# First expert stage: the gate multiplies the input rows, relu goes from PSUM straight to the second product's rows, the bias becomes a weight row, and experts are worked in pairs

## The chip, the core and the metric

The kernel runs on one core of a Trainium2 chip, as one program. The metric is the device time of a launch in microseconds (us). The core has TensorE (PE: matrix products, whose clock is granted at 1.2 or 2.4 GHz), VectorE (DVE), ScalarE (ACT), GpSimd (POOL) and SyncE (SP), which here only issues transfers (DMAs). Each engine runs its own instructions in order and waits on semaphores for the others. SBUF is the memory of 128 partitions that all engines read and write. PSUM is the memory that TensorE writes its products to: eight banks of 128 partitions by 512 f32.

## The reference, cut to what matters

The program is eleven stages of a small model over 8 x 1056 rows of 64 numbers. The fifth, `_L0_ffn_ref`, is a mixture of 16 experts:

```python
gate_logits = x @ gate_w + gate_b                       # 16 logits a row
topk_vals, topk_idx = jax.lax.top_k(gate_logits, 2)
topk_w = jax.nn.softmax(topk_vals, axis=-1)             # two weights a row, both positive
h = jax.nn.relu(jnp.einsum('bsh,ehf->bsef', x, w1) + b1)   # 64 -> 128, each expert
expert_out = jnp.einsum('bsef,efh->bseh', h, w2) + b2      # 128 -> 64
moe = sum over the two chosen experts of weight * expert_out
y = x + moe;  then layer norm with gamma and beta, and the residual
```

Here x is already the layer-normalised input of the stage: its 64 numbers have mean zero in every row.

## The kernel before

The stage is `moe(..., "mo0", relu=True, E=16, ...)`, line 2046. It takes the 8448 rows in MK = 11 blocks of MN = 768 rows. A block is kept as two halves of EN = 384 rows: the 64 numbers of a row of the first half lie on partitions 0 to 63, those of the second half on 64 to 127, the rows along the columns. All experts are computed for all rows; an expert that a row hasn't chosen has weight zero.

For each expert n of a block, four things are done. TensorE makes the hidden numbers (`z`, L2392: two f32 products of 64 rows of weights by 128 columns, 384 columns streamed, one for each half, into two banks). ACT applies relu with the bias b1 and writes `act1` (L2510, 128x768). TensorE spreads the expert's weight over 128 partitions (`spread`, L2427: two bf16 products with a matrix of ones, into banks WB and WB+1). DVE multiplies the two (`g`, L2663, 128x768). Then TensorE multiplies by w2 and adds up over the experts (`down`, L2444, two f32 products of 128 rows of weights by 64 columns, into one bank). In program order TensorE does `up1(n+2)`, `spread(n+1)`, `down(n)`. A block's first expert has six small bf16 products more, for b2 (L2441).

What a block needs besides is placed beside the experts by the table `place`: on DVE the layer norm of the next block (`stats`, `aggregate`, `norm`), its choice of experts (`top`, `gap`, `pick`, `share`, `parts`) and the end of the block before (`add`, `moments`, `end`); on TensorE the turns of rows into columns (`t0` L2357, `w_turn` L2375, `y_turn` L2385) and the logits (L2365); on POOL the roots and the last multiply and adds.

Stages overlap at their ends. While the stage before (`project`, "prj") does its last blocks, SP issues this stage's first loads (`ahead`, which runs `fetch`), on the same queue as that stage's stores. The stage's small constants (`gw`, `sone`, `w2`, `b1`, `b2`) are loaded when SP enters the stage, after the last store of "prj" was issued. In `project`, DVE may write the rows of block b into `hn` only when the store of block b-2 has landed (`back`, L2019), and L1875 is that store. The last expert stage of the program, `expert_units` ("mo1"), has a structure of its own; its lines that matter here are `gates` (L2965, a spread over 64 partitions, 512 columns, both halves into one bank), `third` (L2988) and `gated` (L3151, DVE: input rows times the spread weight).

Of the kernel before, what the change touches and what calls it, by code (L numbers as in the profile page):

```python
# [2045 lines left out]
def moe(nc, a, const, ps, stage, relu, E, h_in, outer, h_out, gate_w, gate_b, norm_w, w1_d, b1_d, w3_d, w2_d, b2_d,  # L2046
        sel_d):
# [3 lines left out]
    hidden = w1_d.shape[1]  # L2051
    NH = -(-hidden // P)
    NW = 1 if relu else 2
    WC = NW * hidden
    E3 = 3 * E
    U = 2
    RING = 2
    assert (U * NH) % RING == 0 and (MK - 3) % U == 0
    if relu:
        place = {"sums": 1, "y_turn": 2, "add": 3, "moments": 4, "end_root": 6, "end": 6, "scale": 7,  # L2060
                 "stats": 0, "aggregate": 1, "root": 3, "norm": 4, "t0": 5, "t0_cp": 6, "logits": 7, "top": 8, "gap": 9,
                 "exp": 11, "pick": 10, "share": 11, "parts": 12, "w_turn": 13, "w_turn_cp": 14}
    else:
        place = {"sums": 1, "y_turn": 1, "add": 2, "end": 4,
                 "stats": 0, "root": 1, "norm": 1, "t0": 3, "t0_cp": 4, "logits": 4, "top": 5, "gap": 5, "exp": 6, "pick": 6,
                 "share": 7, "parts": 7, "w_turn": 8, "w_turn_cp": 9}
    with ExitStack() as ctx:
        nm = Names(nc, ctx, const, stage)
        wf = nm.sb("wf", [P, WC])
        gw = nm.sb("gw", [P, 2, E])  # L2070
        w2 = nm.sb("w2", [P, NH, C])
        sel = nm.sb("sel", [P, NH * P], BF16)
        sone = nm.sb("sone", [P, NH * P])
        iota = nm.sb("iota", [P, E])
        nw = nm.sb("nw", [P, C])
        gb = nm.sb("gb", [P, 2, C])
        gbias = nm.sb("gbias", [P, E])
        b1 = nm.sb("b1", [P, NH])
# [21 lines left out]
        prob = nm.sb("prob", [P, MT, E])  # L2100
        tot = nm.sb("tot", [P, 5, MT])
# [11 lines left out]
        xb = nm.sb("xb", [P, MT, C])  # L2113
# [8 lines left out]
        names = ("blank", "w_in", "gate_in", "vec_in", "rows_in", "e_in", "iota_set", "sel_made",  # L2122
                 "b2_hi", "b2_rest", "st_made", "agg_made", "var_made", "half_set", "rstd_made", "cen_made", "xn_made",
                 "t_mm", "t_cp", "lg_mm", "lg_made", "max_made", "gap_made",
                 "exp_made", "share_made", "stk_made", "wt_mm", "wt_cp", "z_mm", "z3_mm", "wb_mm", "act_made",
                 "sw_made", "g_made", "acc_mm", "y_cp", "yt_mm", "add_made", "end_made", "var2_made", "rstd2_made",
# [4 lines left out]
        WB, SIDE, ACC = 4, 6, 7  # L2131

        def hr(i):
            return min(P, hidden - i * P)

        def steps(eng, step):

            step(0, 0, True, False)
            for it in range(0, (MK - 3) // U):
                for u in range(U):  # L2140
                    step(it * U + (1 + u), (1 + u) % 2, False, False)
            step(MK - 2, MK % 2, False, False)
            step(MK - 1, (MK - 1) % 2, False, True)

        def beside(k, par, first, last, n, end_parts, route_parts):

            for name, part in end_parts:
                if place[name] == n and not first:
                    part(k - 1, 1 - par)
            for name, part in route_parts:  # L2150
                if place[name] == n and not last:
                    part(k + 1, 1 - par)
# [7 lines left out]
        NVEC = 16 * (3 if relu else 1)  # L2160
        NROWS = 16 * (1 + (1 if hidden % P else 0) + (7 if relu else 0))
        NEND = 16 * (2 if relu else 4)
# [1869 lines left out]
```

## Time and profile before

| | |
|---|---|
| median of 3 runs | 2764.04 us (2763.9 to 2764.17) |
| the profiled execution | span 2762.5 us, from its first to its last instruction; 1.5 us less than the median run, which also holds what lies around it |
| share of the span busy | PE 91%, DVE 72%, ACT 54%, POOL 15% |
| the stage | its first hidden product starts at 1362.58 us, its last product ends at about 1720.9 us |
| PE in the stage, 1500 to 1532 us | 31.50 of 32.00 us busy |
| DVE, ACT there | 24.44 and 15.38 of 32.00 us busy |
| granted clock of TensorE | 0.50 until 1368 us, 1.00 from there to the end of the stage |

How to read it: a time is in us from the span's start. A merged row gives the start of the first instruction and the stretch to the end of the last. The ends of products are modelled and overlap the start of the next, so that the distance from one start to the next is the pace, and a busy PE isn't PE at its peak.

### The profile page before, as it was taken

What the parts mean: (1) busy time and instruction counts of PE and PEld (TensorE: products, weight loads), DVE (VectorE), ACT (ScalarE), POOL (GpSimd) and SP (SyncE); (2) the same over time, 40 slices, a digit from 0 to 9 for tenths busy, and PEclk for the clock granted to TensorE, in tenths of its full rate; (3) what the DMA queues carried; (4) which work ended last, traced back from release to release, by engine and by line L of the source; (5) the groups of instructions that cost most, each with busy time, mean ns of one, the idle gap of its engine ahead of it and who ended that gap; (6) DMA issues with size and microseconds to landing.
All of it is one profiled execution on the core that took longest, in us unless ns stands there. A gap on an engine that the chain in (4) does not pass through costs nothing. (4 is left out here: it accounts for less than half of the span.)

```text
span 2762.5 us, 52420 instructions
## 1 busy us (share of the span) xinstructions
PE 2510.6 (91%) x18456; PEld 1101.7 (40%) x18456; DVE 1994.3 (72%) x5104; ACT 1485.0 (54%) x2543; POOL 415.7 (15%) x505
## 2 busy tenths in 40 slices
PE   7887759999999999998699999897789999699999
PEld 3323642333333333333433333566644444433333
DVE  5776769889888988984477776658777675366665
ACT  4322754777777777775144454334756767143443
POOL 1121310000000000003311112223101010411110
PEclk9998767999999999998599999655689999599999
DMA  2001550101010111122500000135532122701110
GB/s 86 16 16 29 179 178 13 34 27 36 25 36 25 36 33 28 36 50 44 115 16 20 18 15 21 47 89 143 189 109 84 63 86 44 151 18 26 31 24 12
DMA packets 233526, 155.21 MB, mean 56 GB/s; under 512 B 187617, under 2 KB 192546, under 8 KB 233042
## 3 DMA queue, kind: packets, MB, share of 16 engines
q1 hardware_dynamic: 220098, 123.57, 16.7%
q0 software_dynamic: 10368, 19.06, 2.4%
q10 hardware_dynamic: 2808, 9.22, 1.5%
q8 instruction: 158, 2.59, 0.4%
q14 instruction: 94, 0.77, 0.1%
HBM read 86.75 MB, written 65.09 MB: 55 GB/s over the span
## 5 line engine op out<-in xcount | busy, mean ns | idle before, releaser
L1758 DVE TENSOR_REDUCE att_mpart<-ps 128x1 f32<-128x512 f32 x1024 | 633.9, 684 | 55.5 <-PE ps L1578 50.4
L1716 ACT ACTIVATE att_p<-ps 128x704 f32<-128x704 f32 x768 | 546.6, 760 | 214.7 <-PE ps L1643 207.6
L1672 PE MATMUL ps<-att_p,att_v 128*9 128x352 f32 x3072 | 300.8, 462 | 0.1
L1578 PE MATMUL ps<-att_kT,att_qT 64*128 64x512 bf16 x1024 | 281.2, 386 | 21.1 <-DMA att_qz<-qt_d 8.4
L1643 PE MATMUL ps<-att_qT,att_kT 64*128 64x352 bf16 x1536 | 251.5, 317 | 7.3 <-ACT att_p L1716 6.9
L1372 DVE TENSOR_REDUCE cau_mpart<-ps 128x1 f32<-128x512 f32 (+5 forms) x384 | 193.2, 553 | 80.8 <-PE ps L1198 60.8
L2510 ACT ACTIVATE mo_act<-ps,mo_b 128x768 f32<-128x768 f32 x176 | 156.3, 901 | 132.3 <-PE ps L2392 128.8
L2663 DVE TENSOR_TENSOR mo_g<-mo_act,ps 128x768 f32<-128x768 f32 x176 | 167.5, 952 | 77.6 <-PE ps L2427 41.5
L1339 ACT ACTIVATE cau_p<-ps 128x704 f32<-128x704 f32 (+6 forms) x272 | 171.5, 660 | 82.4 <-PE ps L1257 49.8
L3062 ACT ACTIVATE mo_act<-ps 128x1024 f32<-128x1024 f32 (+1 forms) x108 | 102.9, 953 | 195.0 <-PE ps L2976 194.7
L1643 PEld LDWEIGHTS ps<-att_qT,att_kT 64*128 64x128 bf16 x1536 | 82.0, 93 | 272.7 <-issue 262.5
L1549 POOL DMA_DIRECT2D o_d<-att_o x128 | 64.1, 508 | 841.1 <-ACT att_o L1699 841.0
L2392 PE MATMUL ps<-mo_x,mo_wf 64*128 64x384 f32 x704 | 162.8, 540 | 0.9 <-issue 0.9
L3173 DVE TENSOR_TENSOR mo_g<-mo_act,ps 128x1024 f32<-128x1024 f32 (+1 forms) x108 | 122.1, 1131 | 50.3 <-PE ps L2988 47.5
L2444 PE MATMUL ps<-mo_g,mo_w 128*64 128x384 f32 x704 | 151.8, 510 | 0.4 <-DVE mo_g L2663 0.4
L1257 PE MATMUL ps<-cau_qT,cau_kT 128*128 128x352 bf16 (+7 forms) x576 | 128.4, 287 | 1.8 <-ACT cau_p L1339 1.5
L1195 PE MATMUL ps<-cau_kT,cau_qT 128*128 128x512 bf16 (+5 forms) x384 | 113.2, 335 | 13.7 <-ACT cau_qT L1314 7.5
L1578 PEld LDWEIGHTS ps<-att_kT,att_qT 64*128 64x128 bf16 x1024 | 87.7, 94 | 93.8 <-issue 53.0
L2988 PE MATMUL ps<-mo_gx,mo_w 64*128 64x512 f32 (+3 forms) x576 | 113.5, 595 | 0.2 <-DVE mo_g L3173 0.2
L599 DVE TENSOR_TENSOR mix_gam<-ps,mix_gamT 128x512 f32<-128x512 f32 x128 | 86.2, 686 | 32.8 <-PE ps L403 32.3
L3000 PE MATMUL ps<-mo_g,mo_w 128*64 128x512 f32 (+1 forms) x432 | 108.8, 582 | 0.4 <-DVE mo_g L3173 0.2
L2976 PE MATMUL ps<-mo_x,mo_w 64*128 64x512 f32 (+1 forms) x432 | 108.8, 581 | 0.0
(448 smaller groups left out, 4271.6 us busy)
## 6 DMA issues: line engine op xcount, KB each, us to landing
qt_d<-pre_qT SPq DMA_DIRECT2D x8, 1056.0 KB, 4.3
kt_d<-pre_kT SPq DMA_DIRECT2D x8, 1056.0 KB, 6.8
att_kT<-kt_d SPq DMA_DIRECT2D x32, 264.0 KB, 2.8
att_qT<-qt_d SPq DMA_DIRECT2D x32, 264.0 KB, 3.0
cqt_d<-cpr_qT SPq DMA_DIRECT2D x8, 1056.0 KB
cau_qT<-cqt_d SPq DMA_DIRECT2D x16, 528.0 KB, 3.9
o_d<-att_o POOLq DMA_DIRECT2D x128, 37.1 KB, 2.7
cv_d<-cpr_v POOLq DMA_DIRECT2D x16, 288.0 KB, 6.0
```

What stands on the lines that cost most here:

```text
L1257: mm = pe.matmul(ps[r0:r0 + kn, at, off:TH], kT[:, u, tile * P:tile * P + kn], qT[:, u, s, q], start=True, stop=m1 <= m0)
L1339: e = act.activation(p[:, n % RING, :, off:TH], ps[:, bank:bank + 2, off:TH], ACT.Exp)
L1372: red = dve.tensor_reduce(mpart[:, j, s, i:i + 1], ps[:, 4 + place, 0:w], AX.X, ALU.max)
L1578: mm = pe.matmul(ps[:, bank, :], qT[half(s), u, j * P:(j + 1) * P], kT[half(s), u, c * BANK:(c + 1) * BANK], start=True, stop=not near)
L1643: mm = pe.matmul(ps[:, bank + s, 0:TH], kT[half(s), u, i * P:(i + 1) * P], qT[half(s), u, cols], start=True, stop=not near)
L1672: mm = pe.matmul(ps[32 * cg:32 * cg + DV, 7, 0:TH], v[:, u, i, s, :], p[:, r, s, :], start=i < 2, stop=i == FULL - 1)
L1716: e = act.activation(p[:, n % PRING, :, :], ps[:, bank:bank + 2, 0:TH], ACT.Exp)
L1758: red = dve.tensor_reduce(mpart[:, j, s, c:c + 1], ps[:, bank, :], AX.X, ALU.max)
L2392: mm = pe.matmul(ps[0:m, bank + s, 0:EN], wf[s * C:(s + 1) * C, w0 + n * P:w0 + n * P + m], x1[s * C:(s + 1) * C, par, :], start=True, sto ...
L2444: mm = pe.matmul(ps[s * C:(s + 1) * C, ACC, 0:EN], w2[0:m, n, :], g[0:m, (par * NH + n) % RING, s, :], start=n == 0 and not relu, stop=n = ...
L2510: act.activation(act1[0:m, r, :, :], ps[0:m, zb:zb + 2, 0:EN], ACT.Relu, bias=b1[0:m, n:n + 1])\
L2663: dve.tensor_tensor(g[0:m, r, :, :], src[0:m, r, :, :], ps[0:m, bank:bank + 2, 0:EN], ALU.mult)\
```

## The change

`moe` is replaced by `relu_units` for this stage. Since the gate weight w of a row is never negative, w * relu(x @ w1 + b1) = relu((w*x) @ w1 + w*b1). So:

- the weight multiplies the 64 input numbers instead of the 128 hidden ones. `gates` spreads it over 64 partitions (48 rows of weights by 64 columns, the two halves of a block into partitions 0 to 63 and 64 to 127 of one bank), for two experts at once, and one DVE instruction (`gated`, 128x768) makes the multiplied rows `gx` of both;
- ACT's relu reads PSUM and writes `g`, which `down` reads: there is no `act1`, no bias operand, and no DVE multiply for each expert;
- b1 enters as a row of the weights. The input's numbers have mean zero, so number 0 is minus the sum of the others: column 0 of `xm` is set to one, w1 rows 1 to 63 get row 0 subtracted, and row 0 is replaced by b1; in the same way for the gate matrix and its bias;
- the loops go over pairs of experts (88 of them). The side work has a table of its own with steps counted in pairs, and bank SIDE is handed round by one order of uses.

```diff
+    place = {"stats": -11, "aggregate": -10, "root": -10, "norm": -9, "t0": -8, "t0_cp": -8, "logits": -7, "top": -7,
+             "gap": -6, "exp": -6, "pick": -5, "share": -5, "parts": -4, "w_turn": -3, "w_turn_cp": -3,
+             "sums": 7, "y_turn": 10, "add": 10, "moments": 11, "end_root": 11, "end": 12, "scale": 12}
...
             for r in (0, C):
-                sp.dma_start(wf[r:r + C, 0:hidden], w1_d).then_inc(S["w_in"], 16)
+                sp.dma_start(w1[r + 1:r + C, :], w1_d[1:C, :]).then_inc(S["w_in"], 16)
+                sp.dma_start(w1[r:r + 1, :], b1_d).then_inc(S["w_in"], 16)
+                sp.dma_start(w0[r + 1:r + C, :], w1_d[0:1, :].broadcast_to([C - 1, E * P])).then_inc(S["w_in"], 16)
...
+            pool.tensor_tensor(gw[:, :, :], gw[:, :, :], g0[:, :, :], ALU.subtract).then_inc(S["gw_made"], 1)
...
+                pool.tensor_tensor(w1[:, cols], w1[:, cols], w0[:, cols], ALU.subtract).then_inc(S["w_made"], 1)
...
+            def gates(m):
+                j, q = divmod(m, PAIRS)
+                if q == 0:
+                    pe.wait_ge(S["side_read"], use_no["w_turn", j] + 1)
+                at_least(pe, S["gx_made"], m)
+                for i in range(2):
+                    e = 2 * q + i
+                    for s in range(2):
+                        mm = pe.matmul(ps[halves(s), GATE + i, 0:EN], sel[s * C:s * C + E3, e * C:(e + 1) * C],
+                                       wT[s * C:s * C + E3, j % 2, :], start=True, stop=True)
+                mm.then_inc(S["gate_mm"], 1)
...
+            def up(m):
+                pe.wait_ge(S["gx_made"], m + 1)
+                for i in range(2):
+                    at_least(pe, S["g_made"], 2 * (m - 1) + i + 1)
...
+                if 0 <= step + 1 < N_PAIRS:
+                    up(step + 1)
+                if 0 <= step + 2 < N_PAIRS:
+                    gates(step + 2)
+                if 0 <= step < N_PAIRS:
+                    down(step)
+                side_parts(step, parts)
...
-                        act.activation(act1[0:m, r, :, :], ps[0:m, zb:zb + 2, 0:EN], ACT.Relu, bias=b1[0:m, n:n + 1])\
-                            .then_inc(S["act_made"], 1)
+                    act.wait_ge(S["z_mm"], 2 * m + i + 1)
+                    act.activation(g[:, m % 2, i, :, :], ps[:, Z[i]:Z[i] + 2, 0:EN], ACT.Relu).then_inc(S["g_made"], 1)
...
-                    dve.tensor_tensor(g[0:m, r, :, :], src[0:m, r, :, :], ps[0:m, bank:bank + 2, 0:EN], ALU.mult)\
-                        .then_inc(S["g_made"], 1)
+                dve.tensor_tensor(gx[:, m % 2, :, :], x1[:, j % 2, :].unsqueeze(1).broadcast_to([P, 2, EN]),
+                                  ps[:, GATE:GATE + 2, 0:EN], ALU.mult).then_inc(S["gx_made"], 1)
```

TensorE's order in the middle of a block, before (two experts; L2392 hidden products, L2427 spread, L2444 second product):

```order
L2392 MATMUL ps<-mo_x,mo_wf 128x384 x2
L2427 MATMUL ps<-mo_wT,mo_sel 128x384 x2
L2444 MATMUL ps<-mo_g,mo_w 64x384 x2
L2392 MATMUL ps<-mo_x,mo_wf 128x384 x2
L2427 MATMUL ps<-mo_wT,mo_sel 128x384 x2
L2444 MATMUL ps<-mo_g,mo_w 64x384 x2
```

The same place now, two pairs, that is four experts (L2378 `up`, L2367 `gates`, L2393 `down`):

```order
L2378 MATMUL ps<-mo_gx,mo_w 128x384 x4
L2367 MATMUL ps<-mo_wT,mo_sel 64x384 x4
L2393 MATMUL ps<-mo_g,mo_w 64x384 x4
L2378 MATMUL ps<-mo_gx,mo_w 128x384 x4
L2367 MATMUL ps<-mo_wT,mo_sel 64x384 x4
```

The hidden and the spreading products of two experts now stand together, and the spreading ones have 64 columns of weights instead of 128.

DVE's order in the middle of a block before, where the choice of experts is worked out (L2566 to L2574 `pick`, L2586 to L2590 `share`):

```order
L2663 TENSOR_TENSOR mo_g<-mo_act,ps 128x768
L2566 CAST mo_idx<-mo_i 128x12
L2568 TENSOR_TENSOR mo_eq<-mo_iota,mo_idx 128x96 x2
L2571 TENSOR_TENSOR mo_mask<-mo_eq 128x96
L2574 TENSOR_TENSOR mo_top<-mo_mask,mo_ex 128x96
L2663 TENSOR_TENSOR mo_g<-mo_act,ps 128x768
L2586 TENSOR_REDUCE mo_tot<-mo_top 128x6
L2589 RECIPROCAL mo_tot<-mo_tot 128x6
L2590 TENSOR_TENSOR mo_wt<-mo_top,mo_tot 128x96
L2663 TENSOR_TENSOR mo_g<-mo_act,ps 128x768
```

And now (`pick`, `share` and the `moments` of the block before, L2552 to L2556, in one step):

```order
L2535 TENSOR_TENSOR mo_gx<-mo_x,ps 128x768
L2499 CAST mo_idx<-mo_i 128x12
L2501 TENSOR_TENSOR mo_eq<-mo_iota,mo_idx 128x96 x2
L2504 TENSOR_TENSOR mo_mask<-mo_eq 128x96
L2506 TENSOR_TENSOR mo_top<-mo_mask,mo_ex 128x96
L2511 TENSOR_REDUCE mo_tot<-mo_top 128x6
L2512 RECIPROCAL mo_tot<-mo_tot 128x6
L2513 TENSOR_TENSOR mo_wt<-mo_top,mo_tot 128x96
L2552 BN_AGGR mo_stats<-mo_bst 128x2 x6
L2555 TENSOR_SCALAR mo_var<-mo_stats 128x6
L2556 TENSOR_TENSOR mo_cen<-mo_y,mo_stats 128x384
L2535 TENSOR_TENSOR mo_gx<-mo_x,ps 128x768
```

Between two of the multiplies that TensorE waits for there are now up to eleven small instructions.

SP's queue at the end of "prj", now (L2161 to L2199 are this stage's first loads, L1875 and L1876 the stores of "prj"):

```order
L2161 DMA mo_h<-hidden_1 128x3x64 x4
L2195 DMA mo_w<-in_L_ffn_w1s 63x2048
L2196 DMA mo_w<-in_L_ffn_b1f 1x2048
L2197 DMA mo_w<-in_L_ffn_w1s 63x2048
L2195 DMA mo_w<-in_L_ffn_w1s 63x2048
L2196 DMA mo_w<-in_L_ffn_b1f 1x2048
L2197 DMA mo_w<-in_L_ffn_w1s 63x2048
L2199 DMA mo_gb<-in_L_ffn_gamma 128x64
L2199 DMA mo_gb<-in_L_ffn_beta 128x64
L1875 DMA hidden<-prj_hn 128x8x64
L1876 DMA hidden<-prj_hn 32x64
```

Before, the six in the middle were two loads of 64x2048 (L2220), and a small one for `gbias`.

## Rows read from the trace of the kernel before

**Rows 1.** Busy time in a stretch: us, engines (instructions), clock, DMA share, GB/s
```profile
1500.00:1532.00 32.00, 31.50 (x181) 11.53 (x178) 24.44 (x79) 15.38 (x20) 6.14 (x5) 1.00 0.09 20
```

**Rows 2.** Timeline of PE, one block, from one `y_turn` to the next
```profile
1500.60 0.55 PE L2385 MATMUL ps<-eye,mo_y 128*128 128x128 f32 x3
1501.08 0.92 PE L2392 MATMUL ps<-mo_x,mo_wf 64*128 64x384 f32 x4
1501.83 0.33 PE L2427 MATMUL ps<-mo_wT,mo_sel 48*128 48x384 bf16 x2
1502.09 0.87 PE L2444 MATMUL ps<-mo_g,mo_w 128*64 128x384 f32 x4
1502.88 0.92 PE L2392 MATMUL ps<-mo_x,mo_wf 64*128 64x384 f32 x4
1503.86 0.34 PE L2427 MATMUL ps<-mo_wT,mo_sel 48*128 48x384 bf16 x2
...
1504.93 0.92 PE L2392 MATMUL ps<-mo_x,mo_wf 64*128 64x384 f32 x4
1506.28 0.34 PE L2427 MATMUL ps<-mo_wT,mo_sel 48*128 48x384 bf16 x2 [0.44 <-DVE mo_g L2663]
...
1532.96 0.55 PE L2385 MATMUL ps<-eye,mo_y 128*128 128x128 f32 x3
```

**Rows 3.** Timeline of DVE and ACT in the same block
```profile
1502.04 0.90 ACT L2510 ACTIVATE mo_act<-ps,mo_b 128x768 f32<-128x768 f32 x1 [1.38 <-PE ps L2392]
1502.78 0.94 DVE L2663 TENSOR_TENSOR mo_g<-mo_act,ps 128x768 f32<-128x768 f32 x1
1503.63 0.50 DVE L2625 BATCH_NORM_AGGREGATE mo_stats<-mo_bst 128x2 f32<-128x6 f32 x6
...
1504.72 0.55 DVE L2209 TENSOR_TENSOR mo_xn<-mo_cen,mo_rstd 128x384 f32<-128x384 f32 x1
...
1516.17 0.17 DVE L2566 CAST mo_idx<-mo_i 128x12 f32<-128x12 uint32 x1
...
1517.42 0.95 DVE L2663 TENSOR_TENSOR mo_g<-mo_act,ps 128x768 f32<-128x768 f32 x1
1518.29 0.25 DVE L2586 TENSOR_REDUCE mo_tot<-mo_top 128x6 f32<-128x96 f32 x1
...
1519.09 0.95 DVE L2663 TENSOR_TENSOR mo_g<-mo_act,ps 128x768 f32<-128x768 f32 x1
```

**Rows 4.** Timeline of the start of the stage, at half clock
```profile
1342.02 0.69 DVE L2019 TENSOR_TENSOR prj_hn<-ps,prj_res 128x512 f32<-128x512 f32 x1 [1.90 <-PE ps L1958]
...
1344.27 0.47 SPq L2251 DMA_DIRECT2D mo_gw<-in_L_ffn_gate_w  x1
...
1355.79 0.26 DVE L2531 TENSOR_TENSOR mo_lg<-ps,mo_gbias 128x96 f32<-128x96 f32 x1 [12.96 <-PE ps L2365]
...
1361.20 0.48 PE L2375 MATMUL ps<-eye,mo_stk 128*128 128x128 bf16 x3 [5.55 <-DVE mo_stk L2602]
...
1362.58 2.93 PE L2392 MATMUL ps<-mo_x,mo_wf 64*128 64x384 f32 x8 [0.90 <-issue]
1365.27 0.56 PE L2427 MATMUL ps<-mo_wT,mo_sel 48*128 48x384 bf16 x2
...
1367.50 0.84 PE L2441 MATMUL ps<-mo_wT,mo_b2s 128*64 128x384 bf16 x6
```

**Rows 5.** Busy time in a stretch, while the weights of this stage load
```profile
1334.00:1336.00 2.00, 2.00 (x14) 1.44 (x12) 0.78 (x3) 0.00 (x0) 0.83 (x5) 0.50 1.06 227
```

**Rows 6.** Timeline of DVE at the end of the last `project` stage, "cpj"
```profile
2396.05 0.69 DVE L2019 TENSOR_TENSOR cpj_hn<-ps,cpj_res 128x512 f32<-128x512 f32 x1 [5.74 <-DMA hidden<-cpj_hn]
```

**Rows 7.** Timeline of the last expert stage, "mo1"
```profile
2444.17 0.40 PE L2965 MATMUL ps<-mo_wT,mo_sel 24*64 24x512 bf16 x2
...
2444.50 1.09 PE L2988 MATMUL ps<-mo_gx,mo_w 64*64 64x512 f32 x8
2444.61 0.69 DVE L3151 TENSOR_TENSOR mo_gx<-mo_x,ps 128x512 f32<-128x512 f32 x1 [0.81 <-PE ps L2965]
```

More of the change, by code:

```diff
@@ L2043, with relu_units @@
 EN = MN // 2
[L2046 to L2066, printed above, removed]
+def relu_units(nc, a, const, ps, stage, h_in, h_out, gate_w, gate_b, w1_d, b1_d, w2_d, b2_d, sel_d):
+    E, E3 = 16, 48
+    PAIRS = E // 2
+    N_PAIRS = MK * PAIRS
+    Z, GATE, SIDE, ACC = (0, 2), 4, 6, 7
+    place = {"stats": -11, "aggregate": -10, "root": -10, "norm": -9, "t0": -8, "t0_cp": -8, "logits": -7, "top": -7,
+             "gap": -6, "exp": -6, "pick": -5, "share": -5, "parts": -4, "w_turn": -3, "w_turn_cp": -3,
+             "sums": 7, "y_turn": 10, "add": 10, "moments": 11, "end_root": 11, "end": 12, "scale": 12}
+    FIRST, LAST = -11, N_PAIRS + 5
+    uses = sorted([(j * PAIRS + place[n], n, j) for n in ("t0", "logits", "w_turn", "y_turn") for j in range(MK)],
+                  key=lambda x: x[0])
+    use_no = {(n, j): i for i, (_, n, j) in enumerate(uses)}
@@ L2130, in moe, with halves, at, side_parts @@
         block = const["block"]
[L2131 to L2152, printed above, removed]
+        def halves(s):
+            return slice(s * C, (s + 1) * C)
+        def at(step, offset):
+            j, rest = divmod(step - offset, PAIRS)
+            return j if rest == 0 and 0 <= j < MK else None
+        def side_parts(step, parts):
+            for name, part in parts:
+                j = at(step, place[name])
+                if j is not None:
+                    part(j)
         def rows_of(d, k, s):
@@ L2282, in step @@
                 end_rows(k)
[L2283 removed]
+                if k > 0:
                     store(k - 1)
[L2286 removed]
             store(MK - 1)
[L2288 to L2289 removed]
         @block.gpsimd
@@ L2448, in _ @@
-            end_parts = (("y_turn", y_turn),)
-            route_parts = (("t0", t0), ("logits", logits), ("w_turn", w_turn))
-            def step(k, par, first, last):
-                for n in range(NH):
-                    two, one = over(k, par, n + 2, last), over(k, par, n + 1, last)
-                    if two:
-                        up1(two)
-                    if one:
-                        spread(one)
-                        if not relu:
-                            up3(one)
-                    down(k, par, n)
-                    beside(k, par, first, last, n, end_parts, route_parts)
```

552 lines of the change are left out of this document (227 added, 325 removed).

## The prediction

> **What bounds the kernel now.** I read the busy time by stretch first, then PE's timeline over one block, DVE's over the same block, the start of the stage, and at the end two other stages that already do something like the new code.
>
> In the middle of the stage PE is busy 31.50 of 32 us, DVE 24.4, ACT 15.4, at full clock [rows 1]. So PE sets the pace, and the question is what PE's time is made of. Its timeline [rows 2] shows an undisturbed expert from 1501.08 to 1502.88: hidden products 0.75 us, spread 0.26, second product 0.79, together 1.80. Two places are longer: from 1502.88 to 1503.86 the hidden products take 0.98, and from 1504.93 to 1506.28 1.35. In both the spread waits until DVE has emptied banks WB with `g`, and DVE is late because it did side work (L2612 on, L2625 to L2209) between two `g`. That is 0.23 + 0.60 = 0.83 us. A block takes 1532.96 - 1500.60 = 32.36 us: 16 x 1.80 = 28.8, the 0.83, and 2.7 of side products and a short wait.
>
> What the 1.80 us is made of matters for the change. 384 columns at 2.4 GHz are 0.16 us, and an f32 product takes four such passes, its two halves side by side: 0.64. The hidden products take 0.11 more, the second ones 0.15 more, the bf16 spread 0.10 more than its one pass [rows 2]. These extras stand where PE goes over to another shape of weights (64x128 and 48x128 count as one shape, 128x64 as another). That they belong to the change of shape, not to every product, is seen at the start of the stage: two experts' hidden products stand together there, at half clock, and take 1365.27 - 1362.58 = 2.69 us for 8 passes of 0.32 = 2.56; the extra is paid once [rows 4].
>
> **Part 1: PE's time for a pair.** Now two experts' products of a kind stand together, but the spread has weights of 48x64 in the corners of the array, a third shape. `up`: 8 passes 1.28, 0.11 on entering, 0.10 on leaving: 1.49. `gates`: 2 passes 0.32, 0.03 entering (bf16 weights are small), 0.10 leaving: 0.45. `down`: 1.28 + 0.15: 1.43. Sum 3.37 us, against 2 x 1.80 = 3.60. Three changes of shape take the place of four. 88 pairs x 0.23 = **20.2 us less**. The bounds: nothing if the corners cost double at each change (3.60), and 0.10 a pair more if the step from `up` to `gates` costs nothing. I take the middle, since the stage "mo1" goes from corner weights (L2965, 512 columns, 0.21 us a pass) to the next products in 2444.50 - 2444.17 = 0.33, that is 0.12 over its pass [rows 7]: an ordinary change.
>
> The Trainium skill (TensorEngine Tiling (Array Packing), Tiling Modes) says that changing the tiling mode drains TensorE. The trace agrees, with the 0.10 to 0.15 us above; by that rule a third mode is paid for, which the 3.37 holds.
>
> **Part 2: DVE's product on PE's path.** Before, DVE's `g` stood between ACT and `down`. Now `gx` stands between `gates(s+2)` and `up(s+2)` of the next step, and only `down(s)` lies between them. From the start of the last `gates` product: until DVE starts 0.44 [rows 7], the product 0.95 for 768 elements from two banks, as for `g` now [rows 3], and to PE 0.14 (L2663 ends at 1503.72, L2427 starts at 1503.86) [rows 2, 3]: 1.53. PE needs 0.26 + 1.43 = 1.69. So it is just hidden, with 0.16 to spare, as long as DVE is free. If it took 1.04 (0.69 for 512 elements in rows 7, scaled) it would still fit.
>
> DVE is free if the side work of a step is shorter than PE's step. Between two `gx` PE's pace allows 3.37 - 0.87 (what a multiply takes from the next instruction, 1502.78 to 1503.63) = 2.5 us. By the new table step 3 of 8 holds `pick` 1.25 (1516.17 to 1517.42), `share` 0.80 and `moments` 1.09: 3.14 [rows 3]. Together with the slack that leaves a stall of about 0.45 us in each block. Step 2 (`gap`, `add`) has about 2.5, and PE's own `y_turn` of 0.48 beside it: none. So 10 blocks x (0.83 - 0.45) = 3.8, and about 2 us at the end of the stage, where PE now waits for `g` in the last two experts while the new relu is one product ahead: **6 us less**, bounds 2 and 10.
>
> ACT does 2 x 0.90 of 3.37 us [rows 3], and its relu of a pair is done before the next pair's products need the banks: nothing. The saved `g` (176 x 0.95 of DVE) is worth nothing beyond the stalls. POOL's extra normalisation is a 128x384 product a block on an engine with 6 of 32 us busy [rows 1].
>
> **Part 3: the start of the stage.** The weights' preload doubles: four loads of 63x2048 f32 (2.06 MB) and two single rows, against two of 64x2048 (1.05 MB). They stand in SP's queue ahead of the store of block 5 of "prj", and DVE may not write block 7 before that store has landed. Before, that wait was not there: L2019 at 1342.02 waited for PE [rows 4]. In "cpj", which has 1.5 MB of preload at that place, the same instruction waited 5.74 us for the store [rows 6]. The loads move 227 GB/s [rows 5]; from 1334.0 the 2.06 MB are done at 1343.1, the store of 0.26 MB at 1344.3: 2.3 us late. That is the low bound. The high bound is a load that isn't dealt to all 16 DMA engines: 63 rows can't be cut in 16 equal parts, the most equal parts up to 16 are 9. At 9/16 of the rate, 128 GB/s, the loads end at 1350.1, the store about 1 us later: 9.2 us late. I take the high bound: the code before splits its loads of 72 rows into 64 and 8, sizes that can be cut by 16 and by 8, and the old load had 64.
>
> The Trainium skill (DMA: Bandwidth & Descriptors, Why a DMA increments its semaphore by 16 and not by 1) states this: a DMA runs on the largest number up to 16 that divides its slowest dimension. No row here shows a load of 63 rows.
>
> From L2019 to the first hidden product it was 20.6 us [rows 4]. Now fewer bytes (sel is halved, b1's load goes), but DVE waits for w2 and b2 before it chooses experts, and splits b2 first: I put 21.2 to the first `gates`, X = 1351.2 + 21.2 = 1372.4. POOL's subtraction of the weights hides in that. Then the pipe fills, at half clock: `gates` 0.65, `gx` 1.2, `up` 2.6, `gates` 0.65, `gx` 1.1, `up` and `gates` at full clock 2: `down(0)` with b2's products at X + 8.2, with 2 `up` and 3 `gates` (4.3 us of full-clock work) behind it. Before, L2441 came at 1367.50 with 3 hidden products and 2 spreads (2.8 us) behind it. So the stage's work starts, in effect, at 1376.3 instead of 1364.7: **11.6 us more** (4.7 by the low bound).
>
> **Sum.** 2762.5 - 20.2 - 6 + 11.6 = 2747.9 us of span. The runs shown are 1.5 us over the profiled span, so **2749 us**, 0.5% less than 2764. After the stage all is as before and only moves.
>
> **Rivals.**
> - The preload is dealt evenly to 16 engines: 6.9 us earlier, **2742**. For it: 63 descriptors could be dealt 4 and 3 to an engine. Against: above.
> - The pair costs PE 3.60 as before, the new shape eating what pairing saves: 20.2 more, and the slack then hides step 3's stall (4.5): **2765**. Against it: the 2.69 us in rows 4 and the 0.33 in rows 7.
> - Slower: the two halves of `gates` go one after the other, because both write one bank (before each half had its own). 2 x 0.16 us more in a pair, 28.2 in all, less the stall of 4.5: **2773**. It makes the kernel slower from 0.30 us a pair on. Against it: L2965 is just such a pair of halves into one bank, and goes on after 0.33 us, where two passes one after the other would be 0.43 alone [rows 7]. The Trainium skill (TensorEngine Tiling (Array Packing), Restrictions and Gotchas) says that different row tiles can't access the same PSUM bank at once, and speaks for this rival; the 0.33 us disagrees, so it gets a small chance.
> - Slower too: `gx`, with an operand repeated for two banks, takes much longer than 0.95. Up to 1.1 it is hidden; from 1.4 on the gain is gone; at 1.6 the time is 2749 + 88 x 0.49 = **2792**.
>
> **Numbers.** Forecast 0.50; even deal 0.25; no gain in the pair 0.10; halves in turn 0.06; slow `gx` 0.04; something not seen 0.05. About 0.2% (5.5 us) is what a measurement of this kernel can tell from no change. Faster: the first two and a part of the last, 0.77. Same: 0.12. Slower: 0.11. The range 2738 to 2762 holds the first two with their bounds (stalls 2 to 10, the start 4.7 to 12, the pair 0.10 better) and a pair that saves half of the 0.23.
>
> **What the new profile would show.** A step of 3.37 us between L2378 rows; `gates` 0.45, `up` 1.49, `down` 1.43; one PE wait on `mo_gx` a block, near the step with L2499 to L2556; L2019 in "prj" waiting for a DMA, until about 1351; the first L2367 near 1372; the stage's last L2393 near 1706. What would make it wrong: `gx` products that start late in more than one step of 8, a DMA rate in the preload other than 128 GB/s, or side work whose chains (choice of experts in the step before `w_turn`) run out of time.

## The result, and the profile after

The first comparison gave 2739.6 us for the changed kernel (4 runs, 2735.96 to 2741.25) against 2764.11 us: a ratio of 0.9903 (0.9876 to 0.993), 24.5 us less by the medians. The forecast was 2749 us, 15 less, with a range down to 2738. The ratio times 2764.04 is 2737.2 us, just under that range. Two more comparisons of the same two kernels, below, gave 0.9961 and 0.9955.

The profiled execution has a span of 2738.9 us. In the middle of the stage DVE's load fell from 24.4 to 17.2 of 32 us and PE stayed full, as before [rows 1]; this is the busy time of the engines in the same stretch of the changed kernel:

```profile
1500.00:1532.00 32.00, 31.75 (x196) 13.33 (x195) 17.21 (x71) 15.21 (x23) 6.96 (x6) 1.00 0.09 19
```

PE's timeline over the first pairs of a block, after `y_turn` (L2354) and up to the next one:

```profile
1507.86 0.55 PE L2354 MATMUL ps<-eye,mo_y 128*128 128x128 f32 x3
1508.34 1.56 PE L2378 MATMUL ps<-mo_gx,mo_w 64*128 64x384 f32 x8
1509.83 0.51 PE L2367 MATMUL ps<-mo_wT,mo_sel 48*64 48x384 bf16 x4
1510.27 1.51 PE L2393 MATMUL ps<-mo_g,mo_w 128*64 128x384 f32 x8
1511.71 1.56 PE L2378 MATMUL ps<-mo_gx,mo_w 64*128 64x384 f32 x8
1513.20 0.51 PE L2367 MATMUL ps<-mo_wT,mo_sel 48*64 48x384 bf16 x4
1513.64 1.51 PE L2393 MATMUL ps<-mo_g,mo_w 128*64 128x384 f32 x8
1515.40 1.56 PE L2378 MATMUL ps<-mo_gx,mo_w 64*128 64x384 f32 x8 [0.25 <-DVE mo_gx L2535]
...
1537.64 0.55 PE L2354 MATMUL ps<-eye,mo_y 128*128 128x128 f32 x3
```

From start to start, a pair takes 3.37 us (1511.71 - 1508.34): `up` 1.49, `gates` 0.44, `down` 1.44. The third pair's `up` comes at 1515.40 instead of 1511.71 + 3.37 = 1515.08: one wait of 0.32 us for `gx`. The block takes 1537.64 - 1507.86 = 29.78 us, against 32.36 before [rows 2].

DVE's timeline shows what that wait is for. The `gx` of 1514.40 stands behind `pick`, `share` and `moments`; each instruction starts within 0.04 us of the end of the one before, so DVE had no pause:

```profile
1510.38 0.96 DVE L2535 TENSOR_TENSOR mo_gx<-mo_x,ps 128x768 f32<-128x768 f32 x1 [0.49 <-PE ps L2367]
...
1513.31 0.51 DVE L2552 BATCH_NORM_AGGREGATE mo_stats<-mo_bst 128x2 f32<-128x6 f32 x6
1513.85 0.17 DVE L2555 TENSOR_SCALAR mo_var<-mo_stats 128x6 f32<-128x6 f32 x1
1513.93 0.55 DVE L2556 TENSOR_TENSOR mo_cen<-mo_y,mo_stats 128x384 f32<-128x384 f32 x1
1514.40 0.95 DVE L2535 TENSOR_TENSOR mo_gx<-mo_x,ps 128x768 f32<-128x768 f32 x1
```

At the start of the stage, against [rows 4], the last block of "prj" waits for its store, and the first `gates` come 22.6 us after it. SPq is SP's DMA queue: the small store L1876 stands there for 6.04 and 3.44 us behind the loads (in the kernel before 0.58 and 0.69 us, at 1336.47 and 1339.95).

```profile
1336.07 6.04 SPq L1876 DMA_DIRECT2D hidden<-prj_hn  x1
...
1343.50 3.44 SPq L1876 DMA_DIRECT2D hidden<-prj_hn  x1
```

```profile
1348.13 0.69 DVE L2019 TENSOR_TENSOR prj_hn<-ps,prj_res 128x512 f32<-128x512 f32 x1 [8.51 <-DMA hidden<-prj_hn]
...
1359.67 1.26 DVE L2578 CAST mo_b2s<-mo_b 128x128 bf16<-128x128 f32 x1 [10.73 <-DMA mo_b<-in_L_ffn_b]
1360.96 2.45 DVE L2581 TENSOR_TENSOR mo_b<-mo_b,mo_b2s 128x128 f32<-128x128 f32 x1
...
1364.30 0.26 DVE L2468 COPY mo_lg<-ps 128x96 f32<-128x96 f32 x1
```

```profile
1370.69 0.85 PE L2367 MATMUL ps<-mo_wT,mo_sel 48*64 48x384 bf16 x4 [0.67 <-ACT mo_wT L2437]
```

### The profile page after: what moved, and what is told of

The parts are those of the page before. It is cut to its first block, busy times and chain, and to the rows that moved or that the text cites. A ratio compares the mean times of both kernels' runs of the same rounds, so it can differ in the third digit from the quotient of the medians.

```text
span 2738.9 us, 51722 instructions
## 1 busy us (share of the span) xinstructions
PE 2474.6 (90%) x18456; PEld 1099.2 (40%) x18456; DVE 1920.0 (70%) x5016; ACT 1464.4 (53%) x2543; POOL 431.3 (16%) x523
## 4 chain that ended last, share of the span: by engine, by line
PE 75%; DVE 11%; ACT 5%; issue 4%; DMA 2%; POOL 2%; SPq 1%; DVEq 0%; ACTq 0%; POOLq 0%
PE ps L1672 10%; PE ps L1578 7%; PE ps L1643 6%; PE ps L2378 4%; PE ps L2891 4%; PE ps L2903 4%; PE ps L2879 3%; PE ps L2393 3%; PE ps L1283 3%; PE ps L1257 3%; PE ps L1668 2%; PE ps L1195 2%; PE ps L403 2%; PE ps L413 1%; PE ps L2367 1%
## 5 line engine op out<-in xcount | busy, mean ns | idle before, releaser
L2451 ACT ACTIVATE mo_g<-ps 128x768 f32<-128x768 f32 x176 | 133.2, 808 | 131.0 <-PE ps L2378 131.0
L2535 DVE TENSOR_TENSOR mo_gx<-mo_x,ps 128x768 f32<-128x768 f32 x88 | 83.9, 954 | 124.4 <-PE ps L2367 124.4
L2378 PE MATMUL ps<-mo_gx,mo_w 64*128 64x384 f32 x704 | 138.7, 513 | 5.6 <-DVE mo_gx L2535 5.6
L2393 PE MATMUL ps<-mo_g,mo_w 128*64 128x384 f32 x704 | 132.2, 497 | 0.0
```

Of the source, the lines that this page charges most:

```text
L2378: mm = pe.matmul(ps[:, Z[i] + s, 0:EN], w1[halves(s), e * P:(e + 1) * P], gx[halves(s), m % 2, i, :], start=True, stop=True)
L2393: mm = pe.matmul(ps[halves(s), ACC, 0:EN], w2[:, 2 * q + i, :], g[:, m % 2, i, s, :], start=False, stop=q == PAIRS - 1 and i == 1)
```

## The experiments

Each kernel was timed beside the kernel before on the same chip, and one execution of it was profiled. Since executions turned out to differ by 9 us and more outside the stage, what an experiment says of the stage is read from its trace, between landmarks that all traces have: the first product of the second stage (L832), DVE's first L2019 in "prj", its last one, the first `gates` (L2367; before, the first spread, L2427), the first product of the linear attention, and that of "lpr" (L1933). Differences of their starts in us (their line numbers shift a little in the edited kernels). The expectations count to the stage's last `down`, whose start lies some 2.6 us ahead of the linear attention's:

| kernel | start to L832 | to first L2019 | to last L2019 | to first gates | to linear attention | to lpr | to the end | first L2019 to linear attention |
|---|---|---|---|---|---|---|---|---|
| before | 263.3 | 1046.8 | 31.98 | 23.25 | 358.01 | 119.8 | 919.4 | 413.24 |
| before_again | 271.5 | 1047.3 | 31.68 | 23.06 | 357.62 | 113.6 | 917.3 | 412.36 |
| before_bytes | 271.7 | 1046.5 | 37.20 | 22.72 | 357.55 | 113.0 | 917.2 | 417.47 |
| after | 262.3 | 1046.1 | 39.77 | 22.56 | 332.78 | 115.1 | 920.3 | 395.11 |
| after_again | 271.0 | 1047.2 | 38.26 | 22.54 | 335.62 | 112.7 | 920.8 | 396.42 |
| after_third | 269.6 | 1046.0 | 39.43 | 22.65 | 332.46 | 114.7 | 920.9 | 394.54 |
| even_rows | 272.8 | 1045.9 | 37.05 | 22.76 | 332.37 | 123.1 | 918.7 | 392.18 |
| five_shapes | 259.9 | 1044.5 | 40.22 | 22.30 | 358.99 | 114.9 | 918.7 | 421.51 |
| moments_later | 261.7 | 1048.4 | 39.75 | 22.49 | 330.44 | 115.7 | 920.3 | 392.68 |
| b2_later | 273.4 | 1047.2 | 40.00 | 19.39 | 334.66 | 115.1 | 920.8 | 394.05 |
| w1_on_dve | 262.5 | 1046.4 | 41.00 | 16.18 | 334.46 | 117.9 | 920.9 | 391.64 |
| all_four | 263.3 | 1044.8 | 36.94 | 16.23 | 330.31 | 115.1 | 920.8 | 383.48 |
| centre_on_pe | 262.4 | 1047.5 | 31.46 | 10.93 | 331.01 | 115.1 | 920.4 | 373.40 |

**Is 24.5 us the change?** Three unchanged kernels: before_again, after_again, after_third.

> The kernel before, unchanged, profiled a second time and timed against itself, as a control. Theory A (what lies outside the changed stage differs between executions by itself): the stretch from the end of lpr back to the start of the linear attention, 120.1 us in the first profile, moves by some us here too, and the stretches of mix and pre move by 1 us or so. Theory B (the new stage leaves the chip in another state, so that its neighbours really are faster after it): every stage here repeats the first profile to a few tenths of a us. The ratio should be 1.000 within 0.002 by both.

> The changed kernel, unchanged, profiled a second time and timed in five rounds. The first comparison gave 0.9903 (0.9876 to 0.993), that is 19 to 34 us less; of the 23.6 us between the profiles 17 came from the stage and its lead-in, 5 from the linear attention, which nobody changed, and 2 from the stages ahead. Theory A (the 5 and the 2 are chance of one execution): another profile gives the linear attention 120 us again, and the ratio settles near 0.993 to 0.994 (17 to 19 us less). Theory B (they belong to the change): 115 us again and a ratio of 0.990 to 0.991. Inside the stage the pair's step should be 3.37 us again, by both.

> The changed kernel a third time, on whichever chip comes, only to narrow the interval: two comparisons gave 0.9903 (0.9876 to 0.993) and 0.9961 (0.9939 to 0.9983). From the first product of prj to the end of the changed stage the four profiles say 429.1 and 428.3 us before, 411.1 and 412.5 after. Theory (the change is worth what these stretches differ by, 16 to 18 us, and the rest of each comparison is the mix of two lengths that token_mix and linear_attn have in either kernel): ratio near 0.994, and the profile shows token_mix ending at about 254 or 264 us, the stretch prj to stage end 411 to 412.5. Rival (the first comparison was right, 24 to 26 us): ratio 0.990 to 0.991.

before_again 1.0003 (0.9979 to 1.0026); after_again 0.9961 (0.9939 to 0.9983); after_third 0.9955 (0.9925 to 0.9985). Neither of the last two is the 0.993 to 0.994 of the expectations; both lie above it, with intervals that reach it. The 35 runs of the kernel before beside the first two went from 2748.88 to 2774.61 us, in lumps near 2754, 2764 and 2773. The table shows where such steps are: the second stage starts at 260 to 263 or at 270 to 273 us with either kernel, and the linear attention takes 113 to 123. The start to L832 moved by 8.2 us between the two profiles of the kernel before, where the expectation had some 1 us. In that stage the clock differs too: PE's granted clock was 0.93 in the stretch from 200 to 256 us of the first profile of before, and 0.87 in the second (columns as in [rows 1]):

```profile
200.00:256.00 56.00, 50.22 (x233) 15.90 (x232) 38.98 (x79) 10.02 (x15) 12.77 (x9) 0.93 0.09 21
```

```profile
200.00:256.00 56.00, 44.24 (x209) 14.33 (x210) 40.81 (x57) 9.33 (x14) 8.01 (x7) 0.87 0.09 21
```

What stays put is the last column: 413.2 and 412.4 before, 395.1, 396.4 and 394.5 after, that is 412.8 - 395.4 = 17.4 us less. Theory A stands for the linear attention: 119.8 us in the first profile of before, 113.6 in the second. The profiles of the first comparison met a long one there in the kernel before and a shorter one in the changed kernel. All 24 runs of the changed kernel have a median of 2748.1 us, all 85 of the kernel before 2763.3: 15.2 less. These runs come from several chips; within the three comparisons the medians differ by 24.5, 12.6 and 13.3 us.

**What is the pair's 0.23 us?**

> In each step TensorE's order becomes up(first expert), gates(first), up(second), gates(second), down(both): the same products, but five changes of the weights' shape in a pair instead of three; gx still has a whole down between the last gates product and the next up. Theory (what pairing saves is changes of shape, 0.10 to 0.17 us each): the step grows from 3.37 to between 3.57 and 3.71 us, so that 88 pairs cost 18 to 30 us more and most or all of the gain is gone (about 2760 to 2770). Rival (the gain comes from DVE's relief, or from the number of products or weight loads, which is the same here): the step stays within 0.05 us of 3.37, the kernel near 2740.

```diff
-                if 0 <= step + 1 < N_PAIRS:
-                    up(step + 1)
-                if 0 <= step + 2 < N_PAIRS:
-                    gates(step + 2)
+                for i in range(2):
+                    if 0 <= step + 1 < N_PAIRS:
+                        up(step + 1, (i,))
+                    if 0 <= step + 2 < N_PAIRS:
+                        gates(step + 2, (i,))
```

Ratio 1.0031 (1.0005 to 1.0056): 0.3% slower than the kernel before. PE's timeline:

```profile
1499.97 0.92 PE L2379 MATMUL ps<-mo_gx,mo_w 64*128 64x384 f32 x4
1500.82 0.35 PE L2367 MATMUL ps<-mo_wT,mo_sel 48*64 48x384 bf16 x2
1501.10 0.92 PE L2379 MATMUL ps<-mo_gx,mo_w 64*128 64x384 f32 x4
1501.94 0.35 PE L2367 MATMUL ps<-mo_wT,mo_sel 48*64 48x384 bf16 x2
1502.22 1.51 PE L2394 MATMUL ps<-mo_g,mo_w 128*64 128x384 f32 x8
1503.66 0.92 PE L2379 MATMUL ps<-mo_gx,mo_w 64*128 64x384 f32 x4
```

A step takes 3.69 us. One expert's `up` takes 0.85 and its `gates` 0.28, two together 1.49 and 0.44: the passes (0.64 and 0.16 for one) are paid for each expert, and 0.21 and 0.12 once for each block of one shape, however long it is. Two more such blocks cost 3.69 - 3.37 = 0.32 us. The same products in another order lose all that pairing gave: the stretch takes 421.5 us, 26 more than in the changed kernel. The theory stands. A rival is that going from f32 to bf16 costs, not the shape, since both change at the same places. It falls with the kernel before: one expert's hidden products there are the same four f32 passes, with bf16 behind them as well, and take 0.75 us (1501.08 to 1501.83 in [rows 2]). The spread behind them has 128 columns of weights; before `gates`, with 64, they take 0.85. So 0.10 us belongs to the other shape.

**Does the side work of one step make the wait?**

> In the table of the changed kernel moments and end_root go from step 11 to 13, end and scale from 12 to 14, so that step 3 of each 8 holds pick and share alone and step 5 holds stats and moments. Theory (the 0.3 us a block that TensorE waits for mo_gx is step 3's side work, 3.14 us in a gap of 2.5): the wait is gone, a block takes 29.45 to 29.55 us instead of 29.78, 2.5 to 3.3 us for the stage. Rival (the wait moves to step 5, where moments now follows stats): the block stays at 29.7 to 29.8.

```diff
-             "sums": 7, "y_turn": 10, "add": 10, "moments": 11, "end_root": 11, "end": 12, "scale": 12}
+             "sums": 7, "y_turn": 10, "add": 10, "moments": 13, "end_root": 13, "end": 14, "scale": 14}
```

```profile
1510.15 0.55 PE L2354 MATMUL ps<-eye,mo_y 128*128 128x128 f32 x3
1510.63 1.56 PE L2378 MATMUL ps<-mo_gx,mo_w 64*128 64x384 f32 x8
1514.01 1.56 PE L2378 MATMUL ps<-mo_gx,mo_w 64*128 64x384 f32 x8
1517.38 1.56 PE L2378 MATMUL ps<-mo_gx,mo_w 64*128 64x384 f32 x8
...
1539.62 0.55 PE L2354 MATMUL ps<-eye,mo_y 128*128 128x128 f32 x3
```

The block takes 29.47 us, and the third pair's `up` follows the second's after 3.37: the wait is gone and has gone nowhere. 395.4 - 392.7 = 2.7 us for the stage (ratio 0.9927, from two runs only).

**Why is the store late: the bytes, or 63 rows?**

> The kernel before with the bytes of the preload doubled and nothing else: each 64x2048 load of the weights is issued twice, the second time into an array that nobody reads (2.1 MB as in the changed kernel, all of 64 rows). Theory (the bytes make the store of prj late, dealt to 9 or to 16 DMA engines): L2019 of prj's last block starts 4 to 6 us later against the first L2019 of prj than in before (32.0 and 31.7 us), so 36 to 38, and the stage ends 4 to 6 us later. Rival (63 rows alone were the cause): it starts within 1.5 us of before.

> The four 63-row loads and the two single rows of the preload become four loads of 64 rows by 2048 (same bytes; b1's row, the zero row and the repeated row 0 stand in the arrays that the launch passes), nothing else in the stage changes but that POOL no longer clears two rows. Theory (a load of 63 rows runs on 9 of the 16 DMA engines and so at 9/16 of the rate): the preload's packets end some 5 us sooner, L2019 of the last block of prj starts 5 to 7 us sooner against the start of prj, the first gates 5 to 7 us sooner, the kernel 5 to 7 us less than after_again (0.2 to 0.25%). Rival (the preload is late because of its bytes, 2.1 MB against 1.05, and their even deal changes nothing): L2019 within 1 us of where it is, and no difference in time.

```diff
                 sp.dma_start(wf[r:r + C, 0:hidden], w1_d).then_inc(S["w_in"], 16)
+                sp.dma_start(dup[r:r + C, 0:hidden], w1_d).then_inc(S["w_in"], 16)
```

```diff
-                sp.dma_start(w1[r + 1:r + C, :], w1_d[1:C, :]).then_inc(S["w_in"], 16)
-                sp.dma_start(w1[r:r + 1, :], b1_d).then_inc(S["w_in"], 16)
-                sp.dma_start(w0[r + 1:r + C, :], w1_d[0:1, :].broadcast_to([C - 1, E * P])).then_inc(S["w_in"], 16)
+                sp.dma_start(w1[r:r + C, :], w1_d).then_inc(S["w_in"], 16)
+                sp.dma_start(w0[r:r + C, :], b1_d).then_inc(S["w_in"], 16)
```

From the first L2019 to the last: 31.8 before, 37.2 with the doubled bytes, 37.05 in even_rows, and 38.3 to 41.0 in the seven profiles that have the changed kernel's preload (mean 39.8). So 5.4 us come from the bytes and 2.7 from the rows; all_four, below, whose preload is cut like that of even_rows, has 36.9. The expectation for even_rows, 5 to 7 us sooner, missed: that 63 rows are the main cause fell. before_bytes ran at 1.002 (1.0 to 1.004), even_rows at 0.9945 (0.9924 to 0.9967). DMA share and GB/s (the last two columns) while the weights load, in the changed kernel:

```profile
1338.00:1340.00 2.00, 1.24 (x12) 0.88 (x10) 1.09 (x1) 0.00 (x0) 1.13 (x2) 0.50 0.57 205
1340.00:1342.00 2.00, 0.00 (x0) 0.00 (x0) 0.00 (x0) 0.00 (x0) 0.00 (x0) 0.50 0.60 176
1342.00:1344.00 2.00, 0.00 (x0) 0.00 (x0) 0.00 (x0) 0.00 (x0) 0.00 (x0) 0.50 0.60 166
```

and in even_rows:

```profile
1348.00:1350.00 2.00, 1.72 (x16) 1.36 (x14) 0.38 (x1) 0.00 (x0) 0.00 (x0) 0.50 1.02 225
1350.00:1352.00 2.00, 0.00 (x0) 0.00 (x0) 0.00 (x0) 0.00 (x0) 0.00 (x0) 0.50 1.04 213
```

A share of 0.57 to 0.60 is 9 of 16 engines (0.56), one of 1.0 all 16. But 9 engines moved 182 GB/s, the mean of the three rows, and 16 moved 219: 0.83 of the rate, not 0.56. Single stretches scatter: other profiles of the 63-row preload have 152 to 221 GB/s in 2 us at a share of 0.57 to 0.62.

**What stands between the last L2019 and the first gates?**

> DVE's splitting of b2 (five instructions on 128x128) moves from ahead of the choice of experts in block 0 to behind its last part; it is needed only by down(0). In the changed kernel it took DVE 4.6 us ahead of the first choice while POOL subtracted the weights (a CAST of 1.26 us and a subtraction of 2.45). Theory 1 (these five stand on the path to the first gates, and are slow because POOL works on SBUF at the same time): the logits' copy (top) starts about 4.5 us sooner after L2019 and first gates 3 to 4.5 us sooner; the small instructions of top and gap, which now meet POOL's subtraction, are slow instead, and the first b2 instruction is quick if POOL has ended. Rival (DVE waits at that place for something that comes at the same time anyway, the b2 rows or the logits): first gates less than 1 us sooner.

> As b2_later, and the subtraction of row 0 from the weights (two instructions on 128x1024) is done by DVE before its first step, where it waits for the gate's constants anyway, instead of by POOL. In b2_later DVE's gap took 2.05 us and its CAST 1.43, where 0.26 and 0.17 are usual, and each ended within 0.1 us of one of POOL's two subtractions (2.38 us each, from 1371.06). Theory (a POOL instruction with two f32 operands in SBUF holds DVE's instruction up until it ends): without them gap takes 0.26 and the CAST 0.17, and from L2019 of the last block of prj to the first gates it is 16.2 to 16.6 us instead of 19.4 (b2_later) and 22.6 (the changed kernel). Rival (the two were slow for another reason, such as the loads that land at that time): they stay slow, 19 us.

```diff
+                if step == place["parts"]:
+                    dve.wait_ge(S["rows_in"], NROWS)
+                    for x in range(3):
...
-            pool.wait_ge(S["w_in"], NW)
-            for s in range(2):
...
+            dve.wait_ge(S["w_in"], NW)
+            for s in range(2):
+                cols = slice(s * E * P // 2, (s + 1) * E * P // 2)
+                dve.tensor_tensor(w1[:, cols], w1[:, cols], w0[:, cols], ALU.subtract).then_inc(S["w_made"], 1)
```

(b2_later has the first piece alone.) The path is 22.6 us in the changed kernel, 19.39 with b2 behind the choice, 16.18 with the subtraction on DVE too. DVE and then POOL in b2_later:

```profile
1371.46 2.05 DVE L2477 TENSOR_TENSOR mo_gap<-mo_lg,mo_m 128x96 f32<-128x96 f32 x1
...
1373.51 0.16 DVE L2480 FIND_INDEX8 mo_i<-mo_m,mo_lg 128x8 uint32<-128x16 f32 x1
...
1374.42 1.43 DVE L2499 CAST mo_idx<-mo_i 128x12 f32<-128x12 uint32 x1
```

```profile
1371.06 4.76 POOL L2307 TENSOR_TENSOR mo_w<-mo_w 128x1024 f32<-128x1024 f32 x2
```

POOL's two instructions end at 1371.06 + 2.38 = 1373.44 and at 1375.82. DVE's subtraction ends at 1373.51 and its CAST at 1375.85: each ended just after one of POOL's. The index searches (FIND_INDEX8) between them took their usual time, while POOL's second one ran. In w1_on_dve the same two are back to normal:

```profile
1360.54 0.26 DVE L2472 TENSOR_TENSOR mo_gap<-mo_lg,mo_m 128x96 f32<-128x96 f32 x1
...
1361.71 0.17 DVE L2494 CAST mo_idx<-mo_i 128x12 f32<-128x12 uint32 x1
```

The theory stands: without POOL's subtraction neither waits. The Trainium skill (SBUF — State Buffer, SBUF: two separate sides) says that VectorE and GpSimd share one port pair to SBUF as an exclusive lock, held for the whole instruction, which a VectorE instruction takes against a GpSimd one that reads SBUF if it has two inputs in SBUF or runs in a two-port mode. The trace agrees, with the ends 0.07 and 0.03 us apart, and for the index searches, which have one input in SBUF; in which mode the CAST ran, no view shows. b2_later ran at 0.9926 (0.9897 to 0.9956), w1_on_dve at 0.9924 (0.9897 to 0.995).

**The edits together, and a preload without the second array.**

> moments_later, b2_later, the subtraction on DVE and the loads of 64 rows together. If the terms add: 3.2 us for the stalls, 3.2 and 3.0 for the start's chain, 2.5 for the loads, so the stretch from the first L2019 of prj to the stage's last down takes 380 to 383 us instead of 391.9 to 393.8, and the median is 10 to 12 us under the changed kernel's: ratio to the kernel before 0.990 to 0.991. Rival (what the chain gains is lost to a clock that rises later after the first gates, as in b2_later, where the first down came 11.4 us behind the first gates instead of 9.2): 384 to 387, ratio near 0.992.

> The second array of weights (row 0 repeated, 1 MB) is not loaded at all: TensorE makes the shifted weights in the idle time before the first gates, by four f32 products of a constant 65x128 matrix (ones on the diagonal, minus ones in row 0, b1 as row 65) with the loaded weights, and ACT copies them out of PSUM. The gate's constants, the spreading matrix and b2 are laid out whole by the launch and loaded with the preload; b2 is split behind the choice, moments moved as in moments_later. The preload has 1.1 MB instead of 2.1. Theory (the start of the stage is bound by the store behind the preload and then by the gate's constants, which are loaded only after it): L2019 of the last block 31.7 to 33 us after the first one instead of 39.6, the first gates 9 to 12 us behind it instead of 22.6, the stretch to the stage's last down 367 to 373 us (392.3 in the changed kernel), ratio 0.985 to 0.988. Rival (the products at half clock stand in the way of the first block's turns, and the clock rises later): 375 to 380, ratio about 0.989.

```diff
+            def centre(i):
+                pe.matmul(ps[:, W_BANK[i], :], small[0:C + 1, 4 * E:4 * E + P], wb[0:C + 1, i * BANK:(i + 1) * BANK],
+                          start=True, stop=True).then_inc(S["w_mm"], 1)
...
+            def centred(i):
+                act.wait_ge(S["w_mm"], i + 1)
+                act.activation(w1[:, i * BANK:(i + 1) * BANK], ps[:, W_BANK[i], :], ACT.Identity).then_inc(S["w_made"], 1)
```

all_four: 0.9902 (0.9869 to 0.9935), stretch 383.5 us. The terms add up: 2.7 for the stalls, 2.7 for the rows and 22.6 - 16.2 = 6.4 for the path to the first `gates`, 395.4 - 2.7 - 2.7 - 6.4 = 383.6. centre_on_pe: 0.987 (0.9838 to 0.9901), 2721.24 us, the fastest kernel of the study. It has more edits than the diff shows: the gate's constants and b2 are laid out whole by the launch and loaded with the preload, and `moments` and the splitting of b2 stand where all_four has them. Its last L2019 is on time again (31.46), and the first `gates` come 10.93 us behind it:

```profile
1341.41 0.69 DVE L2019 TENSOR_TENSOR prj_hn<-ps,prj_res 128x512 f32<-128x512 f32 x1 [2.40 <-DMA hidden<-prj_hn]
```

```profile
1345.62 5.47 PE L2383 MATMUL ps<-mo_wb,mo_small 65*128 65x512 f32 x6
1351.16 0.50 PE L2328 MATMUL ps<-eye,mo_stk 128*128 128x128 bf16 x3
1352.34 0.85 PE L2350 MATMUL ps<-mo_wT,mo_sel 48*64 48x384 bf16 x4 [0.67 <-ACT mo_wT L2431]
```

Three of the four parts of the shifted weights (L2383) are made while DVE chooses experts, and end just as `w_turn` (L2328) is ready to go; the fourth comes behind the first `gates`. That the `gates` come 5.3 us sooner than in all_four is the gate's constants: the logits' products start 2.9 us behind the last L2019 instead of 8.3, where they waited for POOL and the load of the constants. What the missing 1 MB alone is worth is read from the last L2019: 5.5 us sooner than in all_four. The stretch to the linear attention is 373.4 us, 22 less than in the changed kernel.

## Why the prediction was right and wrong

- **The pair.** Forecast 3.37 us, with `up` 1.49, `gates` 0.45, `down` 1.43. Measured 3.37, 1.49, 0.44, 1.44, and five_shapes shows the reason. Both rivals against it (no gain, halves in turn) fell with these numbers, and slow `gx` fell with 0.96 us.
- **The stalls.** Forecast 0.83 down to 0.45 a block, in the step with `pick`, `share` and `moments`. It was that step, with 0.32. The stalls before were mis-sized as well: beside the 0.83, [rows 3] hold a `g` (1517.42) that is late behind `pick`, which I read for its duration only. PE lost 0.13 there, 1518.52 - 1517.64 = 0.88 instead of 0.75, in the kernel before:

```profile
1517.64 0.92 PE L2392 MATMUL ps<-mo_x,mo_wf 64*128 64x384 f32 x4
1518.52 0.34 PE L2427 MATMUL ps<-mo_wT,mo_sel 48*128 48x384 bf16 x2
```

  A block became 32.36 - 29.78 = 2.58 us shorter instead of 8 x 0.23 + 0.38 = 2.22; 0.26 of the 0.36 between them are these two stalls, 0.13 each. Over ten blocks that makes 3.6 us more gain.
- **The start.** L2019 9.2 us late came out at 39.8 - 31.8 = 8.0. "I take the high bound" rested on a step that failed, "At 9/16 of the rate, 128 GB/s": the deal to 9 engines was right, the rate wasn't. The low bound of 2.3 us was wrong as well: even doubled bytes in equal parts gave 5.4. Two errors of opposite sign left a fair number. The even deal as a rival was to be 6.9 us earlier; it is 2.7.
- **From L2019 to the first gates.** Forecast 21.2, measured 22.6. The waits for b2 were seen; what wasn't is that "POOL's subtraction of the weights hides in that" is false: it holds DVE up, by 1.0 and 2.2 us in two instructions (1.26 and 2.45 us against 0.23 and 0.29). Counted as the prediction does, by the start of b2's products in the first `down` (L2389 at 1379.60, 71.2 us behind the first L2019; before, L2441, 57.5 us behind it), less the 1.5 us of work that is further ahead by then, the start costs 12.3 us instead of 11.6.
- **The sum.** From the first L2019 to the linear attention 17.4 us less, forecast 14.6 (20.2 + 6 - 11.6). The 2.8 us between them are mostly the 3.6 of the blocks, less the 0.7 that the start cost more.
- **The number.** The step that failed is "After the stage all is as before and only moves": the sum puts what lies outside the stage at nothing, and gives no reason. Of the 23.6 us between the first two profiles, 5.5 lie there: 4.7 in the linear attention and 1.7 ahead of the first L2019, less 0.9 given back behind. The other 18.1 lie between the first L2019 and the linear attention, 3.5 more than the forecast's 14.6, which is about what the mis-sized stalls make. The two make the 9.0 us that the profiles' difference is over the forecast. The unchanged kernels show the 5.5 to be chance. With it fell "About 0.2% (5.5 us) is what a measurement of this kernel can tell from no change", which was taken from three runs of before within 0.3 us of each other: 85 runs spread over 31 us. The range was too narrow even by the prediction's own bounds: 10 us of stalls (4 less), the even deal (6.9 less) and 0.10 a pair (8.8 less) together give 2749 - 4 - 6.9 - 8.8 = 2729, not 2738. That the forecast of 15 us less meets the 15.2 of all runs is partly luck: the stage gave 2.8 us more than forecast, and what lies behind "lpr", put at nothing too, seems to have taken some 2 back.
- **Left open.** "After the stage all is as before and only moves" isn't quite so. From "lpr" to the end, the three profiles with the old stage have 917.2 to 919.4 us, the ten with the new one 918.7 to 920.9: some 2 us more, spread over "lpr", the two stages of the causal attention and "cpj" (by means 0.5, 0.4, 0.3 and 0.8 us). Three profiles with the old stage are few, and no experiment touched it; that the changed stage ends at another phase of the clock's changes is only a guess.

## What to carry to other kernels

Count changes of weight shape as a cost of their own, 0.12 to 0.21 us for each unbroken row of products of one shape here, and put products of one shape together before saving any product. Add to the price of a multiplied preload the stores that stand behind it in the same queue, and look at which idle engine could make the data instead. Before trusting a difference of 1% between two kernels, compare stage by stage between landmarks in several profiles of each: three runs that agree don't show what the spread is.

## What the runs showed of the hardware

- In the stretches shown, nine DMA engines moved 166 to 205 GB/s with packets of 8 KB, sixteen 213 to 225: a load cut into 9 parts costs much less than 16/9 of the time. The Trainium skill (DMA: Bandwidth & Descriptors, Why a DMA increments its semaphore by 16 and not by 1) says that a DMA runs on the largest number of engines up to 16 that divides its slowest dimension. The trace agrees, with shares of 0.57 to 0.60 for 63 rows and 1.02 to 1.04 for 64, but the number alone says little of the rate.
- A POOL subtraction of 1024 f32 columns (2.38 us) held DVE's CAST and TENSOR_TENSOR until it ended (1.43 and 2.05 us instead of 0.17 and 0.26), but not its index searches (0.16 us each).
- Two products whose weights lie in opposite corners of the array (48 rows by 64 columns) and write the two halves of one PSUM bank ran side by side: four bf16 products of 384 columns took 0.44 us, two passes of 0.16 and 0.12 for the change of shape; one after the other they would take 0.64 for the passes alone.
- The clock rose 6 us after the first `gates` in one profile of the changed kernel and 13 us in another, with the same instructions. In after, PE's granted clock is 0.50 from 1374 to 1376 and 0.90 in the next stretch; in after_again 0.50 from 1390 to 1392:

```profile
1390.00:1392.00 2.00, 2.00 (x12) 0.97 (x10) 0.63 (x1) 0.00 (x0) 0.00 (x0) 0.50 0.03 8
1392.00:1394.00 2.00, 2.00 (x15) 0.93 (x13) 0.00 (x0) 0.49 (x1) 0.00 (x0) 0.98 0.00 0
```

  PE was busy for all of the 2 us ahead of the rise in both (2.00 of 2.00). From the first `gates` to the linear attention it took 332.78 and 335.62 us: 2.8 us of chance in an unchanged kernel. In b2_later and w1_on_dve, whose first `gates` start at 1380.00 and 1366.04, the clock is still 0.50 up to 1390 and up to 1376, and the same stretch takes 334.66 and 334.46 us: so they gave back some of what their shorter path had won.
